# Scores by token on four strips and four banks, and router work at other points of the attention steps

## The chip, the cores and the metric

The kernel runs on one core of a Trainium2 chip. The metric is the device time of one execution in microseconds. Five engines work side by side and meet at semaphores: TensorE (PE: matmuls and transposes into PSUM), VectorE (DVE), ScalarE (ACT), GpSimd (POOL) and SyncE (SP, which issues most DMAs).

## The reference, cut to what matters

A cross-attention block and a mixture of experts, each with a residual, on x of shape (2, 2048, 512):

```python
x = x + xattn(layernorm(x), ctx, ctx, mask, W_out)
x = x + ffn(layernorm(x), proj_w, anchors, routing_temp, w1, w2)

# xattn: 16 heads of 32, 128 keys, mask==0 -> -1e20
energy = einsum('nqhd,nkhd->nhqk', q, k)
attn = softmax(energy / sqrt(512), axis=-1)
out = einsum('nhqk,nkhd->nqhd', attn, v).reshape(N, Q, 512) @ W_out.T

# router: 6 experts, the best 2 of each token
q = tanh(einsum('btd,ed->bte', x, proj_w) / 0.3)
logits = -((6 - einsum('btd,ed->bte', q, anchors)) * 0.5) / clip(routing_temp, 0.1)
top 2 of logits, softmax over the two -> expert_weights
h = gelu(einsum('btd,edh->bteh', x, w1))
out = einsum('bteh,ehd,bte->btd', h, w2, expert_weights)
```

## The kernel before, in words

The 4096 tokens are cut into 8 blocks (`nblk`) of 512, a block into 4 tiles of 128 tokens. Attention comes first, in steps s = -3 to 44; every engine has a function `attention(s)` and a loop over s, and what an engine does in a step, and in which order, is written out by hand there. The steps are a software pipeline: the constants `L_...` say by how many steps a stage lags (`L_TOK` 5, `L_MT` 9, `L_KEY` 10, `L_PV` 11, `L_DIV` 12, `L_SPLIT` 13, `L_MID` 17). A unit is four heads of one block (`unit(v)`: block v // 4, head group v % 4), so that there are 32 units. `quarter(s)` gives i = (s - 17) // 4 and q = (s - 17) % 4; block i is projected in the quarters q = 0 to 3, one tile each. The last step is `S_LAST` = 44; the last block's projection and the experts follow.

What a step does for a unit and a tile:

- Scores by token (`scores_by_token`, lines 1468 to 1485): queries of 128 tokens against the 128 keys, for the maximum over the keys alone (DVE `maxima`, line 1076). Each head is a strip of 32 rows of the array. A product is 128 columns wide and is two records in the trace; a unit has 4 heads x 4 token tiles = 16 products, 32 records. Before the change they run in two pairs of heads: pair 0 behind the scores by key, pair 1 near the end of the step. From unit 6 on (`WIDE`) both pairs use the banks 4 and 5.
- The maxima go, split into a high and a low part by POOL (`nmhl`, lines 751 and 754), through a transpose (line 1621, at q = 0) into `mT`, and from there as extra rows into the scores by key.
- Scores by key (`scores_by_key`, lines 1487 to 1508): keys by 512 tokens in banks 0 to 3, four heads on four strips, minus the maximum; ACT makes the exponentials `prob` (line 909).
- Sums over keys (line 1602, bank 7), weighted values (line 1647, bank 6). ACT takes 1/sum by logarithm and exponential (lines 944, 946), DVE refines it (`newton`, line 1301) and divides (`raw`, line 1314), POOL joins both (`less`, `atT`, lines 762, 766), ACT and POOL split the result in two parts (`atH` 953, `atL` 774).
- New rows are turned for the queries (line 1612, bank 0, ACT `qT`). Output projection of a tile: 12 products (lines 1527 to 1529, bank 3). DVE adds the residual (line 1166) and takes statistics (line 1170, at q = 3 the moments, line 1178); ACT normalises and the rows are turned (line 1541, bank 2, ACT `rows_out`, line 865).
- Router of block i - 2: at q = 1 `logits_part` (1554), at q = 2 `logits` (1563) and ACT `squash` (tanh with two table loads, 892 and 895), at q = 3 DVE `router_logits` (1094 to 1113, ten small operations that wait for each other; `sel` is the last), PE `prefix` (1574, 1577, waits for `sel`), DVE `places` (1125, 1128). At q = 0 of the next block DVE `shares` (1136 to 1158), and POOL scatters the rows to HBM by indirect DMA (723). `z_bank`, `t2_bank` and `out_bank` give the banks: 1, 2 and 3 inside the attention steps.

Each key-score product of a new unit overwrites banks 0 to 3, so the work that borrows such a bank in a step waits for the exponentials that read it (`exp_done`). SP issues loads and stores in the order of the steps too; this order is not touched.

The order of TensorE in a step before: scores by key; scores by token, pair 0; sums; new rows turned; (q = 0) maxima turned; projection; finished rows turned; router product; scores by token, pair 1; weighted values.

The expert stage after step 44 works on tiles of 128 gathered rows and is not touched.

## Time and profile before

| | us |
|---|---|
| median of 3 runs | 670.87 (669.88 to 672.49) |
| profiled execution | 669.76 |
| its span | 668.0 |
| PE busy | 598.8 (90%) |
| DVE busy | 414.5 (62%) |
| ACT busy | 355.4 (53%) |
| POOL busy | 301.4 (45%) |
| mean granted TensorE clock | 0.948 of full |

The span is what the profiler saw between the first and the last instruction; the execution's own time is 1.8 us longer. Times within the trace count from the span's start. A busy TensorE is a modelled one: matmuls overlap, and a group of products is best measured from its start to the start of the next group.

### The profile page before, as it was taken

What the parts mean: (1) busy time and instruction counts of PE and PEld (TensorE: products, weight loads), DVE (VectorE), ACT (ScalarE), POOL (GpSimd) and SP (SyncE); (2) the same over time, 40 slices, a digit from 0 to 9 for tenths busy, and PEclk for the clock granted to TensorE, in tenths of its full rate; (3) what the DMA queues carried; (4) which work ended last, traced back from release to release, by engine and by line L of the source; (5) the groups of instructions that cost most, each with busy time, mean ns of one, the idle gap of its engine ahead of it and who ended that gap; (6) DMA issues with size and microseconds to landing.
All of it is one profiled execution on the core that took longest, in us unless ns stands there. A gap on an engine that the chain in (4) does not pass through costs nothing.

```text
span 668.0 us, 14302 instructions
## 1 busy us (share of the span) xinstructions
PE 598.8 (90%) x4512; PEld 448.9 (67%) x4512; DVE 414.5 (62%) x880; ACT 355.4 (53%) x674; POOL 301.4 (45%) x434
## 2 busy tenths in 40 slices
PE   5789999999999999988897899998999999989950
PEld 3665566666666656654455689897999999978740
DVE  4765766566577567662787945467873346665653
ACT  3636865676584736736768446352344554444420
POOL 4523765646355555456676613224000045645534
PEclk9968999999998979979997799999999999999985
DMA  5411222122212235617365536568576779999986
GB/s 159 128 43 38 80 79 88 58 95 96 96 48 88 91 110 166 213 63 253 128 217 178 220 112 222 188 206 330 172 229 229 224 252 351 394 405 404 382 288 189
DMA packets 60275, 122.09 MB, mean 183 GB/s; under 512 B 7718, under 2 KB 10790, under 8 KB 60204
## 3 DMA queue, kind: packets, MB, share of 16 engines
q1 hardware_dynamic: 49964, 87.61, 39.2%
q0 software_dynamic: 10240, 33.56, 14.0%
q8 instruction: 41, 0.67, 0.5%
q14 instruction: 30, 0.25, 0.1%
HBM read 67.93 MB, written 53.22 MB: 181 GB/s over the span
## 4 chain that ended last, share of the span: by engine, by line
PE 60%; issue 10%; DVE 9%; DMA 9%; POOL 5%; ACT 3%; SPq 3%; POOLq 0%; DVEq 0%; ACTq 0%
PE ps L1482 8%; DMA y_d<-ysb 6%; PE ps L1504 5%; PE ps L1647 4%; PE ps L1527 4%; PE ps L1529 3%; PE ps L1528 3%; PE ps L1702 3%; PE ps L1704 3%; PE ps L1703 3%; PE ps L1728 3%; PE ps L1730 3%; PE ps L1729 3%; PE ps L1688 3%; PE ps L1602 3%
## 5 line engine op out<-in xcount | busy, mean ns | idle before, releaser
L794 POOL DMA_INDIRECT yg<-y_d,y_row x64 | 65.0, 1015 | 129.3 <-DMA y_d<-ysb 73.1
L909 ACT ACTIVATE prob<-ps 128x512 f32<-128x512 f32 x128 | 66.1, 602 | 86.7 <-PE ps L1507 84.0
L1082 DVE TENSOR_REDUCE nmax<-ps 128x4 f32<-128x512 f32 x128 | 82.0, 685 | 46.6 <-PE ps L1482 46.4
L723 POOL DMA_INDIRECT xs_d<-x,to_row x64 | 68.4, 1068 | 71.9 <-DVE to_row L1147 35.5
L1702 PE MATMUL ps<-w1H,xgH 128*128 x276 | 83.7, 303 | 5.0 <-issue 2.7
L1482 PEld LDWEIGHTS ps<-kfT,qT 32*128 32x128 f32 x1024 | 69.9, 200 | 21.0 <-issue 17.9
L1367 DVE TENSOR_TENSOR xgL<-ps,xgH 128x512 fp32r<-128x512 f32 x69 | 47.5, 688 | 55.6 <-ACT xgH L990 51.2
L1482 PE MATMUL ps<-kfT,qT 32*128 32x128 f32 x1024 | 77.3, 292 | 3.6 <-DVE nmax L1082 2.6
L1704 PE MATMUL ps<-w1L,xgH 128*128 x276 | 77.8, 282 | 0.0
L1703 PE MATMUL ps<-w1H,xgL 128*128 x276 | 77.6, 281 | 0.0
L1728 PE MATMUL ps<-w2H,hH 128*128 x138 | 60.3, 437 | 1.1 <-DVE ysb L1380 1.0
L774 POOL TENSOR_TENSOR atL<-atT,atH 128x512 fp32r<-128x512 f32 x32 | 41.2, 1288 | 44.3 <-issue 34.6
L1166 DVE TENSOR_TENSOR x<-ps,x 128x512 f32<-128x512 f32 x32 | 22.0, 689 | 62.3 <-PE ps L1529 62.3
L1527 PE MATMUL ps<-woH,atH 128*128 128x512 f32 x128 | 53.7, 419 | 6.5 <-ACT prob L909 5.0
L1702 PEld LDWEIGHTS ps<-w1H,xgH 128*128 128x128 f32 x276 | 52.4, 190 | 8.5 <-issue 8.4
L1010 ACT ACTIVATE ysb<-ps 128x512 f32<-128x512 f32 x43 | 25.8, 599 | 57.1 <-DMA y_d<-ysb 32.3
L1730 PE MATMUL ps<-w2L,hH 128*128 x138 | 54.5, 395 | 0.0
L1729 PE MATMUL ps<-w2H,hL 128*128 x138 | 54.1, 392 | 0.0
L990 ACT ACTIVATE xgH<-ps 128x512 fp32r<-128x512 f32 x69 | 41.1, 595 | 22.1 <-PE ps L1688 21.5
L1703 PEld LDWEIGHTS ps<-w1H,xgL 128*128 128x128 f32 x276 | 52.7, 191 | 0.0
L1704 PEld LDWEIGHTS ps<-w1L,xgH 128*128 128x128 f32 x276 | 52.3, 190 | 0.0
L766 POOL TENSOR_TENSOR atT<-less,raw 128x512 f32<-128x512 f32 x32 | 41.3, 1292 | 23.7 <-issue 17.7
(212 smaller groups left out, 1329.2 us busy)
## 6 DMA issues: line engine op xcount, KB each, us to landing
xg<-xs_d SPq DMA_DIRECT2D x69, 256.0 KB
y_d<-ysb SPq DMA_DIRECT2D x69, 256.0 KB
xin<-in_x SPq DMA_DIRECT2D x32, 256.0 KB, 2.7
x<-in_x SPq DMA_DIRECT2D x32, 256.0 KB
x_d<-x SPq DMA_DIRECT2D x32, 256.0 KB
x2t<-x_d SPq DMA_DIRECT2D x32, 256.0 KB
out_x<-x2t SPq DMA_DIRECT2D x32, 256.0 KB
w1L<-in_L_ffn_w SPq DMA_DIRECT2D x6, 512.0 KB, 8.2
```

Of the source, the lines that this page charges most:

```text
L723: nc.gpsimd.indirect_dma_start(xs_d, bass.IndirectOffsetOnAxis(ap=to_row[:, n, k, t:t + 1], axis=0), x2[:, n % 4, t, :], None).then_inc(sc ...
L794: nc.gpsimd.indirect_dma_start(yg[:, c % RY, z, :], None, y_d[0:TILES_OF[c // 4] * P, :], bass.IndirectOffsetOnAxis(ap=y_row[:, c, z:z + 1 ...
L909: nc.scalar.activation(prob[v % 2][:, h, :], ps[:, B_SC + h, :], ACT.Exp, scale=scale).then_inc(exp_done, 1)
L1082: nc.vector.tensor_reduce(nmax[:, n % 2, :, g * hpg + h], ps[:, token_bank(v, h), :].rearrange("p (t k) -> p t k", t=4), axis=AX.X, op=ALU ...
L1482: last = mm(ps[:, token_bank(v, h), t * P:(t + 1) * P], qT[n % 3][r:r + HD, g, t * P:(t + 1) * P], kfT[r:r + HD, batch_of(n), g, :], start ...
L1527: mm(o, h[:, g, :], woH[:, g, :], start=(g == 0), stop=False)
L1702: mm(o, xgH[:, p, c, :], w1h[:, cols], start=(c == 0), stop=False)
L1703: mm(o, xgL[:, p, c, :], w1h[:, cols], start=False, stop=False)
L1704: last = mm(o, xgH[:, p, c, :], w1l[:, cols], start=False, stop=(c == kchunks - 1))
L1728: mm(o, hH[:, p, c, :], w2h[:, cols], start=(c == 0), stop=False)
L1729: mm(o, hL[:, p, c, :], w2h[:, cols], start=False, stop=False)
L1730: last = mm(o, hH[:, p, c, :], w2l[:, cols], start=False, stop=(c == halves - 1))
```

## The change: what it does

- `scores_by_token` issues all four heads of a unit in one group, behind the scores by key; `token_bank(h)` is 4 + h, so that banks 6 and 7, which hold weighted values and sums, hold scores too. The group waits for all maxima of the unit before and for newton and raw of the step; sums and weighted values wait for the maximum of the head whose bank they take. The maxima are taken in the order of heads 3, 2, 0, 1.
- `I_OUT`, `I_T2`, `I_Z` become 2, 1, 3 and `B_MT` 3: other banks for projection, turned rows, router and turned maxima.
- PE's order in a step: scores by key; scores by token; new rows turned; finished rows turned; (q = 0) maxima turned; sums; router product; projection; weighted values. Work that borrows a bank waits for its exponential by `unit_left`.
- DVE: raw moves to the head of a step; newton behind the maxima; `router_logits` from q = 3 to the end of q = 2 (behind the residual); `places` before the residual of q = 3; `shares` is cut into `shares_rows` (q = 0) and `shares_gates` (q = 1).
- POOL: the maxima's columns come first, then `row_factors`, then less and atT, then the statistics' factors. ACT: atH first, `rows_out` ahead of the logarithm (at q = 1 behind the exponential), `squash` ahead of normalising, normalising and xn behind the exponential.

The diff, cut to its core:

```diff
-        B_SC, B_XT, B_MT, B_MX, B_NUM, B_DEN = 0, 0, 1, 4, 6, 7
+        B_SC, B_XT, B_MT, B_MX, B_NUM, B_DEN = 0, 0, 3, 4, 6, 7
+
+        TOKEN_ORDER = (3, 2, 0, 1)
...
-        INSIDE, I_OUT, I_T2, I_Z = nblk - 1, 3, 2, 1
+        INSIDE, I_OUT, I_T2, I_Z = nblk - 1, 2, 1, 3
...
-            def maxima(v, pair):
+            def maxima(v, heads):
                 n, g = unit(v)
-                for j in range(2):
-                    h = 2 * pair + j
-                    dve.wait_ge(mx_ready, hpg * v + h + 1)
-                    after(dve, nml_done, n - 1)
+                dve.wait_ge(mx_ready, v + 1)
+                after(dve, nml_done, n - 1)
+                for h in heads:
...
             def attention(s):
+                d = s - L_DIV
+                if live(d, ntile):
+                    dve.wait_ge(rec_done, d + 1)
+                    dve.wait_ge(pv_done, d + 1)
+                    after(dve, at_done, d - 1)
+                    nc.vector.tensor_tensor(raw[:, d % 2, :], ps[:, B_NUM, :], rden[:, d % 2, :], ALU.mult).then_inc(raw_done, 1)
...
+                if live(v, ntile):
+                    maxima(v, TOKEN_ORDER)
+                if q == 0 and live(i - 3, nblk):
+                    shares_rows(i - 3)
+                if q == 1 and live(i - 3, nblk):
+                    shares_gates(i - 3)
...
+                if q == 3 and live(i - 2, nblk):
+                    places(i - 2)
                 if i >= 0:
                     residual(i, q)
+                if q == 2 and live(i - 2, nblk):
+                    router_logits(i - 2)
                 if q == 3:
                     moments(i)
-                    if live(i - 2, nblk):
-                        places(i - 2)
-                if live(v, ntile):
-                    maxima(v, 1)
...
-            def scores_by_token(v, pair):
+            def scores_by_token(v):
...
-                after(pe, mx_done, hpg * (v - 1) + 2 * pair + 2 if v < WIDE else hpg * v + 2 * pair)
+                after(pe, mx_done, hpg * v)
+                after(pe, newton_done, v + L_TOK - L_PV)
+                after(pe, raw_done, v + L_TOK - L_PV)
                 for t in range(4):
-                    for j in range(2):
-                        h = 2 * pair + j
+                    for h in range(hpg):
...
             def attention(s):
                 k = s - L_KEY
+
+                def unit_left(heads):
+
+                    if live(k, ntile):
+                        pe.wait_ge(exp_done, hpg * k + heads)
+
                 if live(k, ntile):
                     scores_by_key(k)
                 a = s - L_TOK
                 if live(a, ntile):
-                    scores_by_token(a, 0)
+                    scores_by_token(a)
...
+                    unit_left(B_MT + 1)
...
                     pe.wait_ge(exp_done, hpg * (v + 1))
-                    pe.wait_ge(mx_done, hpg * WIDE)
+                    if live(a, ntile):
+                        pe.wait_ge(mx_done, hpg * a + TOKEN_ORDER.index(B_DEN - B_MX) + 1)
...
+                if i >= 0:
+                    unit_left(I_OUT + 1)
+                    project(i, q)
+                if rows_twice(s):
+                    w = rows_turned(s)[0] + 1
+                    rows_transposed(w // 4, w % 4)
+
                 if live(v, ntile):
                     b, g = batch_of(unit(v)[0]), unit(v)[1]
+                    if live(a, ntile):
+                        pe.wait_ge(mx_done, hpg * a + TOKEN_ORDER.index(B_NUM - B_MX) + 1)
                     after(pe, raw_done, v)
```

## Rows read from the trace of the kernel before

**Rows 1.** Busy times of two plain steps (PE, PEld, DVE, ACT, POOL, PEclk, DMA share, GB/s)

```profile
142.00:160.00 18.00, 18.00 (x162) 11.75 (x160) 11.57 (x21) 12.38 (x22) 8.69 (x15) 1.00 0.28 89
```

**Rows 2.** Timeline of a step of block 1 (start us, us, engine line op)

```profile
143.11 1.14 PE L1504 MATMUL ps<-qT,kT 32*128 32x512 f32 x8
144.31 1.06 PE L1482 MATMUL ps<-kfT,qT 32*128 32x128 f32 x16
144.50 2.07 ACT L909 ACTIVATE prob<-ps 128x512 f32<-128x512 f32 x4 [2.77 <-PE ps L1507]
145.30 1.06 PE L1602 MATMUL ps<-prob,ones 128*32 128x512 f32 x8
146.29 0.66 PE L1612 MATMUL ps<-ident,xn 128*128 128x128 f32 x4
146.71 0.48 PE L1527 MATMUL ps<-woH,atH 128*128 128x512 f32 x1
...
149.55 0.60 PE L1541 MATMUL ps<-ident,x 128*128 128x128 f32 x4
149.82 0.69 DVE L1166 TENSOR_TENSOR x<-ps,x 128x512 f32<-128x512 f32 x1 [2.54 <-PE ps L1529]
150.08 1.16 PE L1482 MATMUL ps<-kfT,qT 32*128 32x128 f32 x16
150.54 0.70 DVE L1170 BATCH_NORM_STATS2 st<-x 128x6 f32<-128x512 f32 x1
151.17 1.06 PE L1647 MATMUL ps<-prob,ctok 128*32 128x512 f32 x8
151.27 1.29 DVE L1082 TENSOR_REDUCE nmax<-ps 128x4 f32<-128x512 f32 x2
```

**Rows 3.** Timeline: the maxima's transposes at q = 0, step 21

```profile
128.63 0.66 PE L1621 MATMUL ps<-ident,nmhl 128*128 128x128 f32 x4 [0.76 <-POOL nmhl L754]
```

**Rows 4.** Timeline of the ranking and the prefix, steps 32 and 44

```profile
240.76 1.41 DVE L1109 TENSOR_TENSOR gt<-over,thr 128x144 f32<-128x144 f32 x1
...
242.77 0.41 PE L1574 MATMUL ps<-sel,earlier 128*128 128x30 f32 x2 [1.51 <-DVE sel L1113]
...
243.96 0.44 DVE L1178 BATCH_NORM_AGGREGATE mv<-st 128x2 f32<-128x6 f32 x4
...
351.10 0.30 DVE L1094 TENSOR_TENSOR qa<-qr,anc 128x144 f32<-128x144 f32 x1
...
353.67 0.68 DVE L1166 TENSOR_TENSOR x<-ps,x 128x512 f32<-128x512 f32 x1
```

**Rows 5.** By-token scores at half clock, and the stretch behind (columns as in rows 1)

```profile
244.10 2.08 PE L1482 MATMUL ps<-kfT,qT 32*128 32x128 f32 x16
...
244.00:250.00 6.00, 6.00 (x37) 3.09 (x39) 2.59 (x10) 0.00 (x0) 3.55 (x8) 0.50 0.48 158
```

**Rows 6.** Weight loads in flight: slices of by-key, then of by-token scores (us, PEld busy, count)

```profile
234.15:234.20 0.05, 0.03 (x4) 1.00 0.94 369
...
235.45:235.50 0.05, 0.05 (x4) 1.00 0.00 0
```

**Rows 7.** Timeline: starts of the scores by key of steps 17, 28, 32, 36 and 38

```profile
88.24 1.14 PE L1504 MATMUL ps<-qT,kT 32*128 32x512 f32 x8
...
191.40 1.14 PE L1504 MATMUL ps<-qT,kT 32*128 32x512 f32 x8
...
234.17 1.14 PE L1504 MATMUL ps<-qT,kT 32*128 32x512 f32 x8
...
278.58 1.14 PE L1504 MATMUL ps<-qT,kT 32*128 32x512 f32 x8
...
301.14 1.14 PE L1504 MATMUL ps<-qT,kT 32*128 32x512 f32 x8
```

**Rows 8.** Timeline behind step 44: second turned rows, first product of the last block

```profile
356.07 0.76 PE L1541 MATMUL ps<-ident,x 128*128 128x128 f32 x4 [4.02 <-ACT x2T L865]
...
359.55 0.77 PE L1527 MATMUL ps<-woH,atH 128*128 128x512 f32 x1 [0.79 <-DVE used L1128]
```

More of the change, by code:

```diff
@@ L727, in attention @@
             def attention(s):
+                if (s - L_MT) % kchunks == 0 and live((s - L_MT) // kchunks, nblk):
+                    n = (s - L_MT) // kchunks
+                    pool.wait_ge(mx_done, HEADS * (n + 1))
+                    after(pool, mt_ready, n - 1)
+                    columns = nmhl[:, n % 2, :, :].rearrange("p t (h r) -> p t h r", h=hpg)[:, :, :, 0:2 * kchunks]\
+                        .rearrange("p t h (g z) -> p t g h z", z=2)
+                    maxima = nmax[:, n % 2, :, :].rearrange("p t (g h) -> p t g h", g=kchunks)
+                    nc.gpsimd.tensor_scalar(columns[:, :, :, :, 0].bitcast(F32R), maxima, 1.0, None, ALU.mult)\
+                      .then_inc(nmh_done, 1)
+                    pool.wait_ge(nmh_done, n + 1)
+                    nc.gpsimd.tensor_tensor(columns[:, :, :, :, 1].bitcast(F32R), maxima, columns[:, :, :, :, 0],
+                                            ALU.subtract).then_inc(nml_done, 1)
                 i, q = quarter(s)
@@ L730, in attention @@
                     row_factors(i - 1)
+                d = s - L_DIV
+                if live(d, ntile):
+                    n, g = unit(d)
+                    pool.wait_ge(newton_done, d + 1)
+                    after(pool, at_done, d)
+                    nc.gpsimd.tensor_scalar(less[:], newton[:, d % 2, :], -1.0, 2.0, ALU.mult, ALU.add).then_inc(less_done, 1)
+                    pool.wait_ge(less_done, d + 1)
+                    pool.wait_ge(raw_done, d + 1)
+                    after(pool, atL_done, d - 1)
+                    nc.gpsimd.tensor_tensor(atT[:, d % 2, :], less[:], raw[:, d % 2, :], ALU.mult).then_inc(at_done, 1)
                 w = s - L_STAT
@@ L903, in attention @@
             def attention(s):
+                i, q = quarter(s)
+                u = s - L_SPLIT
+                if live(u, ntile):
+                    n, g = unit(u)
+                    act.wait_ge(at_done, u + 1)
+                    after(act, out_ready, 4 * (n - 1))
+                    nc.scalar.activation(atH[:, n % 2, g, :], atT[:, u % 2, :], ACT.Copy).then_inc(atH_done, 1)
                 v = s - L_KEY
@@ L1133, in places, with shares_rows @@
                     nc.vector.tensor_copy(tab_pad[:], used[:, nblk, :]).then_inc(pad_ready, 1)
-            def shares(n):
+            def shares_rows(n):
                 nc.vector.tensor_tensor(pick[:], rank[:].unsqueeze(1).to_broadcast([P, 2, 4, EXPERTS]),
@@ L1148, in shares, with shares_gates @@
                                         0.0, float(rows - 1), ALU.max, ALU.min).then_inc(place_done, 1)
+            def shares_gates(n):
                 dve.wait_ge(wsel_done, n + 1)
@@ L1159, in shares @@
                                         axis=AX.X, op=ALU.add).then_inc(share_done, 1)
+            def shares(n):
+                shares_rows(n)
+                shares_gates(n)
             def residual(n, t):
@@ L1593, in attention @@
                 if live(a, ntile):
-                    scores_by_token(a, 0)
+                    scores_by_token(a)
+                w = s - L_XT
+                if live(w, ntile):
+                    pe.wait_ge(xn_done, w + 1)
+                    after(pe, qT_done, w)
+                    unit_left(B_XT + 1)
+                    for c in range(kchunks):
+                        last = nc.tensor.transpose(ps[:, B_XT, c * P:(c + 1) * P], xn[:, w % 2, c * P:(c + 1) * P], ident[:])
+                    last.then_inc(xt1_ready, 1)
+                i, q = quarter(s)
+                w = rows_turned(s)[0]
+                if live(w, ntile):
+                    unit_left(I_T2 + 1)
+                    rows_transposed(w // 4, w % 4)
+                if (s - L_MT) % kchunks == 0 and live((s - L_MT) // kchunks, nblk):
+                    n = (s - L_MT) // kchunks
+                    pe.wait_ge(nml_done, n + 1)
+                    unit_left(B_MT + 1)
+                    for t in range(4):
+                        last = nc.tensor.transpose(ps[:, B_MT, t * P:(t + 1) * P], nmhl[:, n % 2, t, :], ident[:])
+                    last.then_inc(mt_ready, 1)
                 v = s - L_PV
@@ L1603, in attention @@
                     last.then_inc(sums_ready, 1)
[L1605 to L1632 removed]
+                if q > 0 and live(i - 2, nblk):
+                    unit_left(I_Z + 1)
                 if q == 1:
```

164 lines of the change are left out of this document (52 added, 112 removed).

## The prediction

> **What bounds the kernel now.** I read the page first (TensorE busy 90% of the span), then the busy times of a stretch of two plain steps: TensorE 18.00 of 18.00 us, DVE 11.57, ACT 12.38, POOL 8.69 [rows 1]. A modelled busy time alone proves little, so I laid the timeline of one step beside it (a step of block 1 without router work), start to start [rows 2]: scores by key 1.20 us (143.11 to 144.31), the first pair of scores by token 0.99, sums 0.99, turning of the new rows 0.42, output projection 2.84, turning of the finished rows 0.53, second pair 1.09, and the weighted values, the same form as the sums, 0.99. The sum is 9.05 us, with no gap between groups. So TensorE's order of work is the step, and only what shortens that order, or puts a wait into it, counts. Two other things cost: at q = 0 the maxima's transposes wait 0.76 us for POOL [rows 3], and at q = 3 the prefix products wait 1.51 us for DVE's ranking [rows 4], after which the granted clock is 0.50, the 1.2 GHz level, for some 6.4 us (243.9 to 250.3 by my reading; the 6 us of it in [rows 5] make 3.0 us of lost work). I take 3.2 us for such a fall.
>
> **Scores by token.** Today a unit's 32 matmul records run as twice 16, on two strips each: 0.99 and 1.09 us [rows 2]. The change issues the 32 over four strips. Is a strip's pace the limit, or the pace of issue? By key, on four strips, four weight loads begin within one 50 ns slice; in the two-strip group four are in flight, each of some 187 ns [rows 6]. And the 16 records that take 1.06 us at full clock take 2.08 at half clock [rows 5]: all of it scales with the array's clock. So a strip takes its 8 records in the time that it takes now, and the whole unit costs 1.09, or 1.0 less per step. Bounds: 2.08 (nothing gained) and 0.99; I take 1.09, since the by-key rows are the same kind of load on the same strips.
>
> **The waits that this adds.** Banks 6 and 7 now hold scores and then the weighted values and sums. Let N be the start of the values' group, at the end of a projection. The residual follows 0.27 us behind the projection (149.55 to 149.82), statistics 0.72 later, and the division raw then starts after about 0.60, at N + 1.57 to 1.6; it takes 0.68, and I allow 0.14 for the signal [rows 2]. Only then may the token scores start: N + 2.4. TensorE reaches them at N + 0.99 + 1.20 = 2.19. New wait 0.2 us. Behind it: the first maximum (head 3, bank 7) starts 1.19 after the scores (150.08 to 151.27) and takes 0.65 (half of 1.29), so the sums may start at +2.0; TensorE arrives there at 1.09 + 0.42 + 0.53 = 2.04. No wait. A plain step is 2.4 + 2.04 + 0.99 + 2.84 = 8.27 us against 9.05; without the turned rows (i = 0) 8.23.
> At q = 0 the maxima's transposes sit in bank 3 and wait for all four exponentials, which end 3.46 us after the key scores start (143.11 to 146.57), so they start at N + 0.99 + 3.46 + 0.1 = 4.55 and the sums at 4.96 in place of 4.43: 8.8 us. The wait of 0.76 [rows 3] goes, because POOL does the columns first in its step and all maxima of the block are done by then.
> At q = 1 the router product adds its 0.99 (the form of the sums): 9.3. At q = 2 the folding products add about 0.9: 9.15. On ACT the order within a step changes, not the count: at q = 2 the squashing's table loads stand before normalising and xn, but ACT idles 2.8 us a step ((18.00 - 12.38) / 2 [rows 1]); were it fuller, qT and the key exponentials of the next step would be late, and the transposes behind them. shares_rows and shares_gates lie on DVE between the last maximum, 1.19 + 4 x 0.65 = 3.8 after the scores' start, and newton, which waits for the sums (end at 2.04 + 0.99 = 3.0), then for ACT's logarithm and exponential: some 1.5 us of DVE time in which they are hidden. Without that cover they would push newton and the residual, at most by the 1 us by which gt was held [rows 4]; with the start's 3.2 this is part of A's range below. SP's queue is not touched; POOL's work is reordered alone, and its less and atT of a step come earlier. The scatters stay last there and issue the same DMAs.
>
> **Ranking at q = 2.** The chain of ten small operations takes 2.57 us when it runs free (351.10 to 353.67) and about 4.3 when POOL's 128x512 operations fall into it, as at gt, 1.41 in place of 0.31 [rows 4]. It moves behind the residual of q = 2, which stands right before the next step's raw. So the token scores of q = 3 start at N + 5.0 where TensorE is ready at 2.19: a new idle stretch of 2.8 us. I take 2.6 more for the chain, not 4.3, because POOL's atT waits for that same raw and is still. The prefix no longer waits but takes 1.33 (242.77 to 244.10). So q = 3 is 8.27 + 2.6 + 1.33 = 12.2, and the q = 0 after it 8.8 plus 0.55 for the four moments (0.44 and their signals), 9.35. Queued behind the waiting token scores are the turning of rows, the sums and the projection; ACT waits for them in turn, which is why nothing catches up. I assume that the clock falls here as it falls now: 3.2.
>
> **The sum**, from the starts of key scores [rows 7]:
> Steps 17 to 27, 88.24 to 191.40, 103.2 us: new 33.5 (8.8 + 3 x 8.23) + 33.6 + 27.25 (8.8 + 9.3 + 9.15) = 94.35. Gain 8.8.
> Steps 28 to 31, 42.8: new 12.2 + 9.35 + 9.3 + 9.15 + 3.2 = 43.2. Loss 0.4. Steps 32 to 35, 44.4: gain 1.2. Steps 36 and 37, 22.6: new 12.2 + 3.2 + 9.35 = 24.75, loss 2.2. Together -1.4.
> Steps up to 16: without a projection the loop runs through sums, logarithm, exponential, newton and raw; by my reading that is as long as the step of today. Zero; bounds one stretch of low clock (3.2) either way.
> Steps 38 to 44: no token scores; zero. At the last step the prefix products and places no longer stand between the second turned rows (356.07) and the first product of the last block (359.55) [rows 8]: of 3.5 us some 1.4 remain. Gain 2.1.
> The expert stage starts earlier by the same and is costed at nothing; what hides it is that its weights are in hand: a late weight load would swallow the gain.
> Total 8.8 - 1.4 + 2.1 = 9.5. The profiled execution is 669.76 us, so 660.3; the median of the runs is 1.1 above it: 661.4.
>
> **Rivals.**
> A, the forecast, 661.4. Its own range is 655 to 667: 0.99 or 1.09 a unit (3 us), the ranking at 2.6 or 4.3 (5 us in three places), and the start's 3.2 either way.
> B, the clock holds over the idle stretch at q = 3. Where TensorE waits 1.1 us a step it holds today; at 1.5 with tiny products behind it falls [rows 4, 5]. Three falls fewer: 661.4 - 9.6 = 652.
> C, the hand-over costs more. The loop residual, statistics, raw, scores, maximum, sums, projection is closed, with nothing in hand. If every link costs 0.1 more than I allow, a step is 0.4 longer; over 24 steps this is 9.6: 671, no change.
> D, slower: four strips bring nothing, since matmuls are issued no faster than now. 16 records in 0.99 us are 62 ns each [rows 2]; were this issue, 32 need 2.0, and as the scores stand in the loop, each of the 31 steps from 6 to 36 pays 1.0 more than in A (2.08 against 1.09): 661.4 + 31 = 692. It decides from any pace above 45 ns a record: 32 x 45 ns is 1.44, which takes 0.35 a step, all of A's gain. Against it: the doubling at half clock [rows 5].
> The Trainium skill, page "TensorE: Matmul & The Clock Gate", section Part 1, says that without hardware decode the sequencer spends about 62 ns on a matmul whatever the array's clock, and otherwise starts come no closer than about 25 ns. The first number is exactly the pace above and would make this rival; by the second 32 records could take 0.8. By that rule the pace would not have doubled at half clock, which the trace shows it did.
> E, slower: the idle bits now in every step let the clock fall also at q = 0 and in the steps before 17. Six more falls at 3.2 are 19: 680. It decides where idle time in a step passes about 1.5 us [rows 4]; I expect 0.2 in most.
> That the change doesn't do what it says: the four strips are in the loop as written, so this gets no chance of its own.
>
> **Chances.** A 0.58, B 0.10, C 0.14, D 0.08, E 0.10. Differences below 0.5% (3.4 us) can't be told from no change. Faster: nearly all of A and B, 0.64. Same: C's middle and A's edge, 0.17. Slower: D, E and C's far side, 0.19. The range takes in B below, and C and most of E above: 649 to 678; D is left out.
>
> **What would show it.** In the profile after: a group of 32 token-score records lasting 1.0 to 1.2 us, steps of 8.3 us between key scores at i = 1, no wait before the maxima's transposes for POOL but about 0.5 for ACT, 2.5 to 3 us of idle TensorE before the token scores of steps 28, 32 and 36 with raw as the releaser and 0.50 clock behind it, no wait of the prefix for sel. A group of 2 us would make it wrong by D; steps of 9 us with short groups, by C; clock below 1 in steps 17 to 27, by E.

## The result and the profile after

The changed kernel takes 664.01 us (median of 20 runs, 661.7 to 671.47), the kernel before 670.12 (20 runs, 664.42 to 673.84). The ratio is 0.9942 with a 95% interval of 0.9921 to 0.9964, that is a gain of 3.9 us, between 2.4 and 5.3; the medians alone are 6.1 apart. Forecast was a gain of 9.5, to 661.4. The direction was right and the time lies in the range, but the gain is well under the forecast. The profiled execution took 665.59 us (span 663.9, mean clock 0.942).

The busy times of two plain steps of the changed kernel, and of the stretch of low clock in step 28:

```profile
core 0: us, PE busy (x) PEld busy (x) DVE busy (x) ACT busy (x) POOL busy (x), PEclk, DMA share, GB/s
135.76:152.56 16.80, 16.77 (x161) 9.87 (x161) 11.87 (x21) 12.53 (x22) 8.88 (x15) 1.00 0.30 96
183.70:190.80 7.10, 6.55 (x54) 4.36 (x54) 3.67 (x7) 2.06 (x4) 4.49 (x8) 0.53 0.05 18
```

Two plain steps take 16.80 us where [rows 1] had 18.00 us for nearly the same two (9.05 each). TensorE is still the bound: 16.77 of 16.80 us. The first plain step, to be laid beside [rows 2]:

```profile
135.76 1.09 PE L1522 MATMUL ps<-qT,kT 32*128 32x512 f32 x5
136.19 0.67 DVE L1312 TENSOR_TENSOR raw<-ps,rden 128x512 f32<-128x512 f32 x1
137.01 1.17 PE L1501 MATMUL ps<-kfT,qT 32*128 32x128 f32 x32
138.11 0.66 PE L1626 MATMUL ps<-ident,xn 128*128 128x128 f32 x4
138.24 2.48 DVE L1093 TENSOR_REDUCE nmax<-ps 128x4 f32<-128x512 f32 x4 [0.56 <-PE ps L1501]
139.14 1.06 PE L1650 MATMUL ps<-prob,ones 128*32 128x512 f32 x8
140.13 0.50 PE L1545 MATMUL ps<-woH,atH 128*128 128x512 f32 x1
...
143.08 1.06 PE L1675 MATMUL ps<-prob,ctok 128*32 128x512 f32 x8
144.16 0.71 PE L1522 MATMUL ps<-qT,kT 32*128 32x512 f32 x4
```

All 32 records of a unit now stand in one group of 1.10 us, start to start (137.01 to 138.11). Forecast was 1.09. The profile shows no wait of TensorE before the group, but raw ends only 0.15 ahead of it (at 136.86), and the group starts 1.25 after the key scores; in steps 27 and 31, where raw ends 0.21 ahead, it starts after 1.16 or 1.17. So raw holds the group up by 0.09, where I had 0.2. TensorE's own work is longer than forecast in three places: from the projection's start to the weighted values 2.95 us (140.13 to 143.08; 2.84 in [rows 2], where other work followed the projection), from the values to the next key scores 1.08 (0.99), and the turning of the new rows 0.50 (0.42). At q = 0 (step 21) there is a wait of 0.35, and none for GpSimd in front of the maxima's transposes, where [rows 3] had 0.76:

```profile
119.87 1.17 PE L1501 MATMUL ps<-kfT,qT 32*128 32x128 f32 x32 [0.35 <-DVE raw L1312]
120.97 0.66 PE L1626 MATMUL ps<-ident,xn 128*128 128x128 f32 x4
121.76 0.63 PE L1640 MATMUL ps<-ident,nmhl 128*128 128x128 f32 x4
```

Step 28, the first with the ranking in front of raw. This is the timeline of VectorE (two rows of the ten of the ranking) and TensorE:

```profile
180.84 0.29 DVE L1105 TENSOR_TENSOR qa<-qr,anc 128x144 f32<-128x144 f32 x1
...
183.31 0.18 DVE L1124 TENSOR_SCALAR sel<-rank 128x24 f32<-128x24 f32 x1
183.42 0.69 DVE L1312 TENSOR_TENSOR raw<-ps,rden 128x512 f32<-128x512 f32 x1
...
184.25 2.09 PE L1501 MATMUL ps<-kfT,qT 32*128 32x128 f32 x32 [2.34 <-DVE raw L1312]
186.27 1.11 PE L1626 MATMUL ps<-ident,xn 128*128 128x128 f32 x4
187.18 1.06 PE L1559 MATMUL ps<-ident,x 128*128 128x128 f32 x4
```

The chain takes 2.58 us (180.84 to 183.42), the forecast's bare 2.57; TensorE is idle 2.34 us, and the work behind takes about double until about 190.3: the granted clock of 183.7 to 190.8 is 0.53, near the 1.2 GHz level. Up to here the changed kernel does what the prediction said.

The tail of attention does not. Step 44, DVE and then TensorE:

```profile
339.99 2.02 DVE L1105 TENSOR_TENSOR qa<-qr,anc 128x144 f32<-128x144 f32 x1
...
344.34 0.18 DVE L1124 TENSOR_SCALAR sel<-rank 128x24 f32<-128x24 f32 x1
...
334.17 0.80 PE L1545 MATMUL ps<-woH,atH 128*128 128x512 f32 x1 [1.99 <-DVE x L1183]
...
344.57 0.64 PE L1592 MATMUL ps<-sel,earlier 128*128 128x30 f32 x2 [5.37 <-DVE sel L1124]
...
346.73 0.77 PE L1545 MATMUL ps<-woH,atH 128*128 128x512 f32 x1
...
351.43 0.60 PE L1559 MATMUL ps<-ident,x 128*128 128x128 f32 x4
...
352.91 0.47 PE L1545 MATMUL ps<-woH,atH 128*128 128x512 f32 x1 [0.88 <-ACT x2T L868]
```

The prefix products now stand ahead of the last inside projection, and TensorE waits 5.37 us for the ranking with that projection (346.73) queued behind. In the kernel before, the projection of step 44 came first, and the ranking (from 351.10 on, [rows 4]) ran while TensorE waited for the second turned rows, 4.02 us [rows 8]:

```profile
348.61 0.47 PE L1527 MATMUL ps<-woH,atH 128*128 128x512 f32 x1
...
356.62 0.47 PE L1574 MATMUL ps<-sel,earlier 128*128 128x30 f32 x2
```

The part that I forecast did come: from the second turned rows to the last block's first product it is 1.48 us (351.43 to 352.91) in place of 3.5, where I had 1.4. More is lost ahead of it. From the start of step 41 to the last block's first product it is 36.60 us after and 31.03 before, 5.6 more. The waits that the profile shows in this stretch are 1.11, 0.86, 0.73, 4.02 and 0.79 before, together 7.5, and 1.12, 1.99, 5.37 and 0.88 after, together 9.4. That is 1.9 of it. Most of the rest is the clock, 0.95 of full over the stretch before and 0.86 after: the long wait stands ahead of the projection, which then runs at half clock (records 0.42 apart from 347.30 on, against 0.23) and takes 4.70 us (346.73 to 351.43) in place of 2.84, and the projection of step 43, behind the wait of 1.99, takes 4.21 (334.17 to 338.38) in place of 2.86.

I cut the span at four points that every profile shows. Both kernels were profiled three times in all (two more below, each with nothing edited), which the clock's variation makes necessary:

| us | before, three profiles | mean | after, three profiles | mean | gain | forecast |
|---|---|---|---|---|---|---|
| start to step 17 | 88.24, 89.38, 85.11 | 87.6 | 83.91, 83.41, 82.55 | 83.3 | 4.3 | 0 (±3.2) |
| step 17 to 38 | 212.90, 212.58, 211.12 | 212.2 | 204.76, 203.28, 206.23 | 204.8 | 7.4 | 7.4 |
| step 38 to last block | 58.41, 58.46, 58.81 | 58.6 | 64.24, 62.92, 64.16 | 63.8 | -5.2 | +2.1 |
| last block to end | 308.45, 310.18, 313.26 | 310.6 | 310.99, 309.99, 311.26 | 310.7 | -0.1 | 0 |
| sum | | 669.0 | | 662.6 | 6.4 | 9.5 |

### The profile page after: what moved, and what is told of

The parts are those of the page before. It is cut to its first block, busy times and chain, and to the rows that moved or that the text cites. A ratio compares the mean times of both kernels' runs of the same rounds, so it can differ in the third digit from the quotient of the medians.

```text
span 663.9 us, 14289 instructions
## 1 busy us (share of the span) xinstructions
PE 576.0 (87%) x4512; PEld 422.0 (64%) x4512; DVE 412.2 (62%) x880; ACT 358.3 (54%) x674; POOL 300.0 (45%) x434
## 4 chain that ended last, share of the span: by engine, by line
PE 64%; DVE 10%; DMA 10%; issue 8%; ACT 4%; POOL 3%; SPq 1%; POOLq 0%; DVEq 0%; ACTq 0%
DMA y_d<-ysb 8%; PE ps L1650 5%; PE ps L1545 5%; PE ps L1501 4%; PE ps L1546 4%; PE ps L1547 4%; PE ps L1730 4%; PE ps L1522 4%; PE ps L1732 4%; PE ps L1731 4%; PE ps L1756 3%; PE ps L1758 3%; PE ps L1757 3%; PE ps L1716 3%; PE ps L1675 3%
## 5 line engine op out<-in xcount | busy, mean ns | idle before, releaser
L727 POOL DMA_INDIRECT xs_d<-x,to_row x64 | 65.8, 1028 | 73.6 <-DVE to_row L1158 38.6
L1093 DVE TENSOR_REDUCE nmax<-ps 128x4 f32<-128x512 f32 x128 | 79.5, 684 | 27.2 <-PE ps L1501 27.2
L1501 PEld LDWEIGHTS ps<-kfT,qT 32*128 32x128 f32 x1024 | 35.3, 200 | 34.8 <-issue 34.4
L1501 PE MATMUL ps<-kfT,qT 32*128 32x128 f32 x1024 | 40.3, 296 | 19.3 <-DVE raw L1312 11.4
L1546 PE MATMUL ps<-woL,atH 128*128 128x512 f32 x128 | 51.6, 403 | 0.0
L1547 PE MATMUL ps<-woH,atL 128*128 128x512 f32 x128 | 51.5, 402 | 0.0
```

The source lines that it names most:

```text
L1093: nc.vector.tensor_reduce(nmax[:, n % 2, :, g * hpg + h], ps[:, token_bank(h), :].rearrange("p (t k) -> p t k", t=4), axis=AX.X, op=ALU.ma ...
L1501: last = mm(ps[:, token_bank(h), t * P:(t + 1) * P], qT[n % 3][r:r + HD, g, t * P:(t + 1) * P], kfT[r:r + HD, batch_of(n), g, :], start=Tr ...
L1546: mm(o, h[:, g, :], woL[:, g, :], start=False, stop=False)
L1547: last = mm(o, l[:, g, :], woH[:, g, :], start=False, stop=(g == kchunks - 1))
```

## The experiments

The time of each is compared with runs of the kernel before on the same chip (medians 671.1, 669.1 and 670.4 us in the three timed batches). The runs of one kernel in a batch spread over 1 to 17 us (r_e3 has one of 679.55 beside five up to 658.82), so I lean on where the profile puts the time and on the ratio second.

**Pairs of strips again (e1_pairs).** The changed kernel, but the 32 records in two pairs of heads, one behind the other, still in one place and four banks.

```diff
-                for t in range(4):
-                    for h in range(hpg):
+                for pair in range(2):
+                  for t in range(4):
+                    for h in (2 * pair, 2 * pair + 1):
```

> The changed kernel, with the scores by token issued as two pairs of strips one behind the other (2 x 16 records) in the same place, same banks, same waits. Theory (a strip's own pace is the limit): the group grows from 1.1 to 2.1 us, every step that holds one by 1.0, so 31 x 1.0 = about +31 us on the changed kernel's 664, some 692 to 696. Rival (the pace is that of issue, and the gain of the steps comes from the new order of work alone): the group stays 1.1 to 1.2 us and the time within 2 us of 664.

Measured: 684.8 us, ratio 1.0217 (1.0156 to 1.0278). The group and the next one:

```profile
157.25 1.72 PE L1502 MATMUL ps<-kfT,qT 32*128 32x128 f32 x32
158.90 0.55 PE L1627 MATMUL ps<-ident,xn 128*128 128x128 f32 x3
```

1.65 us start to start, 52 ns a record; on four strips it is 1.10 us, 34 ns. A plain step takes 8.95 in place of 8.40, and steps 17 to 38 210.6 in place of 204.8. So the four strips themselves carry most of the gain of the steps: with the other moves alone they would have brought 1.6 us. The forecast of this run (a group of 2.1 us, 692 to 696 us) was too high, its rival (1.1 to 1.2 us, 664) too low. The starts of the single records in the traces say why. At full clock the records of one strip start 112 ns apart in the kernel before and here, where two strips work at a time, and in the changed kernel, where four do (the first two of a strip can lie further apart); at half clock it is 213 ns (in the kernel before at 244.10, in the changed one at 184.25). So a strip has a pace of its own. The two pairs cost less than twice 1.09 since records of the second pair start while the first still runs.

What I had not expected is the start: step 17 comes at 101.38, 18 us later, with a mean clock of 0.65 over the first 60 us (0.86 in the changed kernel). I have no cause for it that a run shows.

The Trainium skill, page "TensorE: Matmul & The Clock Gate", section Part 1, has a sequencer pace of about 62 ns a matmul without hardware decode. These rows go below it, at 52 and 34 ns, so it doesn't bind here, and rival D, which rested on such a pace, falls.

**The last step alone (e2_last_prefix).** At step 44 prefix behind the projection, places behind residual and moments; every other step as changed.

```diff
-                if q == 3 and live(i - 2, nblk):
+                if q == 3 and s < S_LAST and live(i - 2, nblk):
                     places(i - 2)
...
-                if q == 3:
+                if q == 3 and s < S_LAST:
                     prefix(i - 2)
                 if i >= 0:
                     unit_left(I_OUT + 1)
                     project(i, q)
+                if s == S_LAST:
+                    prefix(i - 2)
```

> The changed kernel, with the prefix products of step 44 behind that step's projection and the places behind the residual, all other steps untouched. Theory (the changed kernel loses at its last attention step because the prefix stands before the projection and waits 5.4 us for the ranking): that projection starts some 5 us earlier, half clock there goes or shrinks, and 3 to 5 us come back: about 660. Rival (the lead is swallowed by whatever comes next, the weights' lower parts on DVE or the expert stage): within 1 us of 664.

Measured: 665.25 us (12 runs), ratio 0.9942 (0.9901 to 0.9983). In the profile the wait for sel falls from 5.37 to 2.01 us and costs no projection:

```profile
341.28 0.41 PE L1594 MATMUL ps<-sel,earlier 128*128 128x30 f32 x2 [2.01 <-DVE sel L1124]
345.77 0.76 PE L1547 MATMUL ps<-woH,atH 128*128 128x512 f32 x1 [2.72 <-DVE used L1139]
```

Step 38 to the last block takes 58.93 us, as in the kernel before (58.6): about 5 us of the tail are this order. The time didn't follow: it is at the changed kernel's ratio, as the rival of this run said, and not at 660. The repeat below takes this up.

**Ranking behind the maxima (e3_rank_early).** The ranking at q = 3, behind the maxima, where VectorE has slack; prefix behind the projection and places behind the moments, at all steps.

```diff
                 if live(v, ntile):
                     maxima(v, TOKEN_ORDER)
+                if q == 3 and live(i - 2, nblk):
+                    router_logits(i - 2)
...
-                if q == 3 and live(i - 2, nblk):
-                    places(i - 2)
                 if i >= 0:
                     residual(i, q)
-                if q == 2 and live(i - 2, nblk):
-                    router_logits(i - 2)
                 if q == 3:
                     moments(i)
+                    if live(i - 2, nblk):
+                        places(i - 2)
...
-                if q == 3:
-                    prefix(i - 2)
                 if i >= 0:
                     unit_left(I_OUT + 1)
                     project(i, q)
+                if q == 3:
+                    prefix(i - 2)
```

> The changed kernel, with the ranking at q = 3 between the maxima and newton, the prefix behind the projection and the places behind residual and moments, in all steps. Theory (ranking in front of raw makes TensorE idle 2.3 us and halves its clock at steps 28, 32 and 36, and again at 44): steps 28, 32 and 36 fall from 14.9, 13.7 and 13.3 us to 9.6 to 10, no half clock there, 3 x 4 us, and 3 to 5 more at the end: 647 to 652. Rival (the ranking then delays newton and the residual, and the stall moves there): those steps at 11 to 12 us, 656 to 660.

Measured: 659.1 us, ratio 0.9845 (0.9796 to 0.9895).

```profile
181.37 2.49 DVE L1093 TENSOR_REDUCE nmax<-ps 128x4 f32<-128x512 f32 x4 [0.56 <-PE ps L1501]
183.78 0.59 DVE L1105 TENSOR_TENSOR qa<-qr,anc 128x144 f32<-128x144 f32 x1
...
186.79 0.41 PE L1592 MATMUL ps<-sel,earlier 128*128 128x30 f32 x2 [0.50 <-DVE sel L1124]
```

TensorE waits 0.50 us for sel, the clock stays full in these steps, and steps 28, 32 and 36 take 10.54, 10.55 and 10.66 us where the changed kernel had 14.90, 13.71 and 13.27: 10.1 us over the three. The forecast had 9.6 to 10 and the rival 11 to 12, so both missed. In step 37 the clock falls all the same (10.74 us). The tail still costs 62.76.

**GpSimd's order alone (e4_pool_first).** The kernel before, with only the splitting of the maxima put at the head of GpSimd's step.

```diff
             def attention(s):
+                if (s - L_MT) % kchunks == 0 and live((s - L_MT) // kchunks, nblk):
+                    n = (s - L_MT) // kchunks
+                    pool.wait_ge(mx_done, HEADS * (n + 1))
...
                 i, q = quarter(s)
                 if q == 0:
                     row_factors(i - 1)
...
-                if (s - L_MT) % kchunks == 0 and live((s - L_MT) // kchunks, nblk):
-                    n = (s - L_MT) // kchunks
-                    pool.wait_ge(mx_done, HEADS * (n + 1))
```

> The kernel before, with only POOL's order changed: the maxima's columns first in a step, ahead of the row factors and the statistics' factors. Theory (the 0.5 to 0.8 us that the maxima's transposes wait for POOL at each q = 0 is on the path): 7 such steps, 4 to 6 us faster than before, about 665, the steps 13, 17, 21 and 25 shorter by 0.6 to 0.9. Rival (what is saved there is lost again at the next wait): the time of before within 1.5 us.

Measured: 664.36 us, ratio 0.9897 (0.9832 to 0.9962), within the noise of the whole change. TensorE's transposes of the maxima wait for nothing:

```profile
122.24 0.66 PE L1611 MATMUL ps<-ident,xn 128*128 128x128 f32 x4
122.73 0.60 PE L1620 MATMUL ps<-ident,nmhl 128*128 128x128 f32 x4
```

Steps 17, 21 and 25 take 9.06, 9.26 and 9.46 (before 9.75, 10.24, 10.27), 2.5 us over the three. The theory of this run (4 to 6 us, about 665) is met in the time, but the steps show only part of it: steps 17 to 38 take 210.05, 2.2 less than the mean before, and step 13 takes 6.29 in place of 6.79. The rest of its lead (step 17 at 83.95) lies in the start, most of it in step 11, which takes 5.85 us here and in one profile of the kernel before, but 9.03 and 9.05 in its two others.

**GpSimd's order of before in the changed kernel (e7_pool_back).** The opposite test: row factors and statistics' factors ahead of the splitting again.

```diff
             def attention(s):
+                i, q = quarter(s)
+                if q == 0:
+                    row_factors(i - 1)
+                w = s - L_STAT
...
                 if (s - L_MT) % kchunks == 0 and live((s - L_MT) // kchunks, nblk):
...
-                i, q = quarter(s)
-                if q == 0:
-                    row_factors(i - 1)
```

> The changed kernel with GpSimd's order of the kernel before: the row factors and the statistics' factors ahead of the splitting of the maxima, at all steps. Theory (in the kernel before the wait of the mask's transposes for the split maxima cost 0.7 to 1.0 us at each step with q = 0, and moving it alone brought 6 us by e4_pool_first, more than those steps add up to): steps 17, 21 and 25 take 0.5 to 1 us more than 9.34, 9.12 and 9.24, the plain steps stay 8.3 to 8.4 and the whole is 2 to 6 us longer, 666 to 670 us. Rival (with the scores in one group the split maxima come early enough in either order): steps with q = 0 within 0.2 us and the time within 1 us of the changed kernel's.

Measured: 675.31 us, ratio 1.0105 (1.0056 to 1.0153), 11 us over the changed kernel's 664.3 in that batch.

```profile
127.23 0.66 PE L1640 MATMUL ps<-ident,nmhl 128*128 128x128 f32 x4 [2.18 <-POOL nmhl L758]
...
163.68 1.04 PE L1640 MATMUL ps<-ident,nmhl 128*128 128x128 f32 x4 [1.76 <-POOL nmhl L758]
164.65 1.94 PE L1650 MATMUL ps<-prob,ones 128*32 128x512 f32 x8
```

```profile
164.00:170.88 6.88, 6.87 (x32) 3.15 (x31) 1.56 (x3) 3.77 (x6) 2.72 (x3) 0.77 0.00 0
```

With the old order GpSimd's row factors go first, and they wait for VectorE's moments. In step 21 these factors start 1.1 us after the step (122.70 - 121.57), in the kernel before at its start (123.87 - 123.84), and TensorE reaches the transposes 3.5 us after the step in place of 4.0. So the split maxima come later and are wanted earlier: 2.18 and 1.76 us of waiting (steps 21 and 25), and after the second one the clock falls. In step 32 of this kernel, on the other hand, the clock stays full behind the 2.34 us of waiting for raw, and the step takes 12.13 us:

```profile
237.19 1.17 PE L1501 MATMUL ps<-kfT,qT 32*128 32x128 f32 x32 [2.34 <-DVE raw L1312]
```

Steps 17, 21 and 25 take 10.65, 11.21 and 12.82. So this part of the change is no detail: without it the change is slower than the kernel before. The loss is larger than this run's forecast had it (666 to 670 us).

**Products to fill the idle time (e6_filler).** Nine products nobody reads, put where TensorE waits for raw. They prevent the idle time without making raw come earlier. They run in steps 28, 32 and 36 alone (27 records in the trace): the edit sits in the token scores, which steps 40 and 44 don't have.

```diff
                 after(pe, mx_done, hpg * v)
+                i, q = quarter(v + L_TOK)
+                if q == 3 and live(i - 2, nblk):
+                    for z in range(9):
+                        mm(ps[:, B_MX, :], woH[:, 0, 0:P], woL[:, 0, :], start=True, stop=True)
                 after(pe, newton_done, v + L_TOK - L_PV)
```

> The changed kernel with nine products of 128 x 512 into a bank that is free, put between the key scores and the score group by token of the steps 28, 32, 36, 40 and 44, where TensorE waits for VectorE's raw behind the ranking (2.34 us in the changed kernel's step 28). The products are used by nobody. Nine of them fill about 1.9 us. Theory (the idle time itself costs 2.3 us a step and the fall of the clock behind it another 3 or so): the granted clock stays 1.00 over steps 28 and 32, these steps take 11 to 12.3 us (14.90 and 13.71 in the changed kernel), and the whole is 4 to 8 us shorter, 656 to 660 us. Rival (the clock falls for another cause than the idle time, or its fall costs nothing since other engines set the step): steps 28 and 32 stay at 13.5 to 15 us and the time at 664.

Measured: 656.99 us, ratio 0.9831 (0.9782 to 0.988), 7.3 us under the changed kernel beside it.

```profile
180.62 2.34 PE L1499 MATMUL ps<-woL,woH 128*128 128x512 f32 x9
183.03 1.17 PE L1505 MATMUL ps<-kfT,qT 32*128 32x128 f32 x32
```

The token scores start 3.7 us after the step in both kernels (183.03 - 179.32; 184.25 - 180.55), so the wait is untouched. But the group takes 1.17 in place of 2.09, the clock is 1.00 from 178 to 250 us (0.93 before this edit), and steps 28, 32 and 36 take 12.14, 12.13 and 12.08. The changed kernel has 14.90, 13.71 and 13.27 in its first profile, and in its two others 13.69, 14.94, 13.27 and 13.71, 13.49, 17.47. So a fall of the clock costs 1.2 to 2.8 us inside the step, and once 5.4, depending on how long the half clock lasts. Step 37 took 10.71 in the first profile and 9.14 here: it has a fall of its own there, which e3_rank_early shows too (10.74), with no idle time before raw. Over steps 17 to 38 it is 197.7 against 204.8, so 7.1 us for three places, 2.4 each on the mean of the profiles and 1.8 to 2.8 in the single ones; the forecast had 3.2. Time and steps came out as the theory of this run said.

**Early ranking and the last step as before (e5_combined).** The edits of e3_rank_early, but block 4 is still ranked at the end of step 43.

```diff
-                if q == 3 and live(i - 2, nblk):
+                if q == 3 and s < S_LAST and live(i - 2, nblk):
                     router_logits(i - 2)
...
+                if s == S_LAST - 1:
+                    router_logits(i - 2)
```

> The changed kernel with the ranking at q = 3 behind the maxima, the prefix behind the projection and the places behind residual and moments at all steps but the last, where the ranking of block 4 stays at the end of step 43 as in the changed kernel, and only prefix and places stand behind projection and residual. Theory (the ranking in the bare place costs the steps 28, 32 and 36, and the last step has a separate price for the ranking behind its maxima): steps 28, 32 and 36 10.5 to 10.7 us as in e3_rank_early, clock 1.00 from 178 to 250 us, and the last block's first product 31 to 32 us after step 41 where e3_rank_early had 34.96 and e2_last_prefix 31.26; so 3 to 4 us shorter than e3_rank_early to the last block, 655 to 657 us, ratio 0.975 to 0.983. Rival (what the last step gains, the expert stage takes back, as with e2_last_prefix): the last block comes earlier, but the time stays 658 to 660.

Measured: 648.63 us, ratio 0.9711 (0.9672 to 0.975), the best of the study. Steps 28, 32 and 36 take 10.53, 10.55 and 10.67; step 38 to the last block 59.49. The forecast had 655 to 657; the repeat below gave 654.1. The clock did not stay quite full (step 29 took 10.32).

**The kernels again, unchanged (c_after, c_before, c_before2).**

> The changed kernel again, beside the others of this batch, nothing edited. Theory (the steps of attention give about 8 us, the tail of attention and the expert stage give part of it back): within 2 us of 664, ratio to the kernel before 0.990 to 0.996, and from the start of step 17 on the same lengths of steps as in its first profile within 0.1 us each; the length of the start may differ, since the granted clock of the first 60 us differed between profiles of kernels with the same start. Rival (the lengths of the steps around the clock falls are chance): steps 28, 32 and 36 come out more than 1 us away from 14.90, 13.71 and 13.27.

> The kernel before again, nothing edited, for a second profile. Theory (the half clock between 49.3 and 56 us, which made step 11 9.03 us long, belongs to the kernel before and comes again): step 11 8 to 9 us, step 17 starts at 87 to 89 us, against 83.4 to 83.9 in the profiles of the changed kernel. Rival (the clock of the start is chance; GpSimd's order moved alone had step 11 at 5.85): step 11 5.2 to 5.9 us, and step 17 at 84.5 to 86 us. From step 17 to 38 212.9 us in either case, within 1.

> As c_before, a third profile of the kernel before: the same two answers stand for step 11. With the first it tells whether the clock of the start differs from run to run of one kernel.

Measured: c_after 664.3 us, ratio 0.9947 (0.9916 to 0.9978); the kernels before 672.32 and 670.08 in one execution each. c_after met the forecast of its time, but not that of its steps: 28 and 32 took 13.69 and 14.94, so which of them carries the longer fall changes from run to run, as the rival said. Step 11 of the kernel before took 9.03, 9.05 and 5.85: the theory that the half clock there belongs to the kernel falls too, it is the luck of a run. Even without it step 17 starts at 85.11, 1.8 us behind the changed kernel's mean.

**The same edits once more, on one chip (r_after, r_e2, r_e3, r_e5).** The batches left open whether the last step's length shows in the time.

> The changed kernel once more, as the base of this batch. 662 to 666 us, ratio 0.990 to 0.996; from step 38 to the last block's first product 62.5 to 64.5 us.

> The kernel of e2_last_prefix again: prefix behind the projection and places behind residual and moments at the last step alone. Theory (what the last step loses shows in the time, and the equal medians of the first batch were chance of the clock): 3 to 5 us under r_after, and 58.5 to 60 us from step 38 to the last block. Rival (what waits behind it in the expert stage, another engine or the clock, takes it back): within 1.5 us of r_after though the last block starts 4 us or more earlier.

> The kernel of e3_rank_early again. 656 to 660 us; from step 38 to the last block 62.5 to 63.5 us.

> The kernel of e5_combined again. Theory (the last step shows in the time): 3 to 4.5 us under r_e3, at a ratio to the kernel before of 0.970 to 0.980. Rival (taken back): within 1.5 us of r_e3. A distance of 9 us as between the two batches would say that the last step is worth more than its own length.

| | us | ratio (95%) | step 38 to last block | last block to end |
|---|---|---|---|---|
| r_after | 666.63 | 0.9955 (0.9926 to 0.9983) | 64.16 | 311.3 |
| r_e2 | 663.68 | 0.9867 (0.9802 to 0.9933) | 58.93 | 313.9 |
| r_e3 | 653.07 | 0.9709 (0.9648 to 0.977) | 62.79 | 311.1 |
| r_e5 | 654.1 | 0.9757 (0.9713 to 0.9801) | 59.48 | 315.2 |

The edit of the last step shortens the tail by 5.2 and 3.3 us, to a tenth as in the first batches (e2_last_prefix 58.93, e3_rank_early 62.76, e5_combined 59.49). In the time it gave 3.0 us here in the first pair and -1.0 in the second; between the earlier batches it was about 0 and 10. On the mean of the four it is 0.004 in the ratio, about 3 us, but single pairs lie between -0.005 and +0.013. The profiles point at the expert stage. From the last block to the end, both profiles of the kernel with the last step's order alone take 314 us (314.2 and 313.9), against 311 of the changed kernel; but the two of e5_combined's kernel take 307.8 and 315.2, and the three of the kernel before 308.5 to 313.3. Part of this lies ahead of the first output tile of the experts: it is done 31.2 us after the last block's first product in e5_combined and 33.9 in r_e5, 33.8 in both profiles of e2_last_prefix's kernel, 33.0 to 33.3 in the changed one. So what the last step gains can be given back there, but the same kernel does it in one run and not in another. Neither theory nor rival stands alone; I leave it open.

The rank of the variants is not open: early ranking is at 0.971 to 0.985 in all four runs that have it, the changed kernel at 0.994 to 0.996.

## Why the prediction was right and wrong

**Right: token scores.** "The whole unit costs 1.09": 1.10. Undone alone (e1_pairs) it costs 0.55 us a step. That the pace of issue was not the limit is shown by 34 ns a record. That a strip's own pace was, is shown by the 112 ns from one record of a strip to its next, with two strips at work as with four.

**Right: the steps.** Plain steps 8.40 and 8.30 (8.27 and 8.23 forecast), q = 0 9.12 (8.8), q = 1 9.42 (9.3), q = 2 9.33 (9.15). Each is 0.1 to 0.3 longer than forecast, so steps 17 to 27 gained 6.5 us and not 8.8 (96.64 in place of 94.35). The plain step shows where: 0.11 between projection and values, 0.09 between values and key scores, 0.08 in the turning of the new rows, all on TensorE itself. The hand-over of C is not where it lies: its wait was 0.09, where I had 0.2. At q = 0 the sums start 4.16 after the key scores (118.15 to 122.31) where I had 3.97.

**Right, with two sizes off: the ranking.** The chain bare at 2.58, the idle time 2.34 (2.8 forecast) and the fall of the clock at all three places, in all three profiles. A fall costs about 2.4 (3.2 forecast), by e6_filler. Both were too dear: steps 28 to 37 take 108.12 us against 109.74, a gain of 1.6 where I had a loss of 1.4. By luck this balances the line above: 6.5 + 1.6 = 8.1 in this profile, and 7.4 over three, against 7.4.

**Wrong: "At the last step the prefix products and places no longer stand between the second turned rows and the first product of the last block ... Gain 2.1", and with it "Steps 38 to 44: no token scores; zero".** The gap that I named did shrink, from 3.5 to 1.48 us; but over steps 38 to the last block the measured sum is a loss of 5.2 us. I followed the prefix out of its old place and did not look at its new one: ahead of the projection. Inside the loop the ranking is long done by then. At step 44 it is not, since VectorE does the ranking of block 4 at the end of step 43 and there are no token scores left to give it time; TensorE waits 5.37 us, the projection waits behind it and then runs at half clock. My own rule, to name what is queued behind a new wait, was kept for the token scores and not here. e2_last_prefix shows it: with this one order put back the stretch is at 58.93, that of the kernel before. How much of it reaches the time stays open, as said above.

**Wrong: the start, "zero; bounds one stretch of low clock either way".** It gained 4.3 us by three profiles each, beyond the bound. The sum of the steps finds it. Up to step 10 both kernels take the same (43.2 and 43.4 us on the mean). Step 10 took 6.16 in all three profiles before, and 5.16, 5.65 and 4.01 after, at different clocks: 1.2 us. Step 11 took 9.03, 9.05 and 5.85 before, and 5.25, 5.19 and 5.02 after: 2.8 us, of which the half clock in two of the profiles before is luck; at full clock it is 5.85 against 5.02. Step 13 took 6.79 and 6.25, and 6.29 in e4_pool_first, so this 0.5 is GpSimd's order. The other steps up to 16 are as long as before (5.86 and 5.88), as I had assumed. So at least 1.3 us of the 4.3 are the change's and some 2 us the luck of the clock; the rest, in step 10, isn't settled. My assumption came from a reading without rows, and it left out the wait for GpSimd at q = 0, which I had priced for the later steps.

**The sum.** 0 + 7.4 + 2.1 + 0 was forecast; 4.3 + 7.4 - 5.2 - 0.1 was measured. These are gains between profiles, 6.4 in all; the timed runs give 3.9 by the ratio and 6.1 by the medians. With the tail as forecast the gain would have been larger than forecast, by the start.

**The rivals.** B, the clock holds: no, it fell at all three places in all three profiles of the changed kernel. But it is not ruled out in general: behind the same 2.3 us of waiting for raw the clock held in step 32 of e7_pool_back and in steps 28 and 36 of e1_pairs. e6_filler shows what B would have brought, 657 where I had 652. D is refuted by the pace. E did not come in the changed kernel, but e7_pool_back is E: idle 1.76 and 2.18 at q = 0, a fall of the clock behind the first of these, and slower than before. "It decides where idle time in a step passes about 1.5 us" held for the fall behind 1.76; the 2.18 of step 21 was followed by plain steps at full clock (8.48 and 8.40), so the idle time alone does not decide.

**What a better reading would have said.** The gain of the change is from strips and from GpSimd's order. The new place of the ranking is no worse than the old one (steps 28 to 37 gained 1.6 us), but a better one was at hand: behind the maxima it brings about 10 us more in the steps, by e3_rank_early.

## What to carry to other kernels

When a hand-written order moves an operation, look it up in its new place at the first and the last turn of the loop as well as in a steady one: what hides it in the middle (here the token scores) may not be there at the end. A long chain of small operations belongs behind the work the critical engine is waiting for, not in front of it; here the same ten operations cost TensorE 2.3 us of idle time a block and its clock about 2.4 more in front of raw, and 0.5 us behind the maxima. And a new order on one engine may need a new order on another: over steps 17 to 38 the same reordering of GpSimd was worth 2.2 us in the old kernel and 9.9 in the new one (one profile each against the mean of three).

## What the runs showed of the hardware

- Idle time of 2.3 us in steps 28, 32 and 36 of the changed kernel cost TensorE about as much again by the clock (2.4 on the mean). Nine idle products in that gap brought 7 us over three places (656.99 against 664.3), with the wait itself unchanged. In 3 of the 21 such steps of all profiles the clock stayed full (steps 28 and 36 of e1_pairs, 32 of e7_pool_back), and in step 37 of e3_rank_early it fell without such a wait.
- Weight loads and products of 32 rows by 128 columns start 112 ns apart on one strip at full clock, with two or four strips at work, and 213 ns apart at half clock. A unit's 32 records cost 34 ns each on four strips, 52 in two pairs (e1_pairs), and 63 on four strips at half clock (184.25 to 186.27).
- VectorE's qa took 2.02 us in step 44 and 0.29 in step 28. Beside the long one GpSimd issued an indirect DMA and ran a 128x512 operation:

```profile
339.58 0.96 POOL L727 DMA_INDIRECT xs_d<-x,to_row  x1 [0.30 <-issue]
340.56 1.27 POOL L778 TENSOR_TENSOR atL<-atT,atH 128x512 fp32r<-128x512 f32 x1
```

  qa ends at 342.01, 0.18 after atL. The Trainium skill, page "SBUF — State Buffer", section "Who interferes with whom", says that a VectorE instruction with two SBUF inputs contends with a GpSimd instruction that reads SBUF, and that the lock on the shared ports is exclusive. The rows agree in that qa, with its two inputs, does not end before atL has; why it gave way though it is noted as begun first, they don't show.
- At the entry of the expert stage, where TensorE has idle time in all, the clock stayed full in e5_combined and fell in the changed kernel, which there took 33.1 us from the last block to the first output tile, against 31.2. The fall alone doesn't explain it: in the kernel before the clock fell there too (0.67 and 0.50 over 375.55 to 383.55), and it took 31.2. A cause was not tried.
